# Depthwise convolution of two channel blocks on TensorE, one more C product on VectorE and a single buffer for step size times x, in the state-space layer of a decoder kernel

## What is computed

```
h = _rms(x, norm_w[i])
xz = jnp.einsum('bld,ed->ble', h, W_in[i])
xi, z = jnp.split(xz, 2, axis=-1)
xp = jnp.pad(xi, ((0, 0), (dc - 1, 0), (0, 0)))
xc = conv_b[i] + sum((xp[:, k:k + L, :] * conv_w[i][:, k] for k in range(dc)))
xc = _silu(xc)
dbc = jnp.einsum('bld,ed->ble', xc, W_x[i])
delta, Bm, Cm = jnp.split(dbc, [rk, rk + n], axis=-1)
delta = jax.nn.softplus(jnp.einsum('blr,dr->bld', delta, W_dt[i]) + b_dt[i])
deltaA = jnp.exp(delta[..., None] * A)
BX = (delta * xc)[..., None] * Bm[:, :, None, :]
_, hs = jax.lax.associative_scan(combine, (deltaA, BX), axis=1)
y = jnp.einsum('bldn,bln->bld', hs, Cm) + D[i] * xc
out = jnp.einsum('bld,ed->ble', y * _silu(z), W_out[i])
x = x + out
```

## Time and profile before

| | us |
|---|---|
| median of three runs | 1399.4 |
| profiled execution | 1391.54 |
| span of the profiled execution | 1389.8 |
| state-space stage in it | 380 to 1077 |

### The profile page before, as it was taken

One profiled execution on the slowest core, in us unless ns is written; L12 is line 12 of the kernel. 1 busy time (PEld: TensorE's weight loads), 2 busy tenths in 40 slices (PEclk: granted clock), 3 DMA queues, 4 the chain that ended last, 5 costly groups with the idle time before them and its releaser, 6 DMA issues.

```text
span 1389.8 us, 17376 instructions
## 1 busy us (share of the span) xinstructions
PE 1138.0 (82%) x5946; PEld 665.0 (48%) x5946; DVE 1119.4 (81%) x1662; ACT 791.7 (57%) x1749; POOL 862.7 (62%) x745
## 2 busy tenths in 40 slices
PE   6688888878579898987988889888787788888774
PEld 2455555544234454544545445454443455556544
DVE  3677777575699999999999999999999167876558
ACT  1355555564367567666676666766653056566653
POOL 4700000100499898998989989999898245445404
PEclk9799999988779899999999999999999889999975
DMA  6000002000510504106041060320500300010000
GB/s 210 11 12 12 12 12 68 1 1 3 196 37 22 210 0 167 40 1 232 0 146 61 1 231 1 116 90 0 191 1 0 107 16 16 17 31 2 1 0 24
DMA packets 21028, 79.88 MB, mean 57 GB/s; under 512 B 4273, under 2 KB 7417, under 8 KB 19961
## 3 DMA queue, kind: packets, MB, share of 16 engines
q1 hardware_dynamic: 20942, 78.79, 16.4%
HBM read 77.55 MB, written 1.23 MB: 57 GB/s over the span
## 4 chain that ended last, share of the span: by engine, by line
PE 29%; POOL 29%; DVE 26%; ACT 9%; issue 5%; DMA 1%; SPq 0%; DVEq 0%; POOLq 0%; ACTq 0%
PE ps L522 27%; POOL arena L1586 17%; POOL arena L1598 9%; DVE ps L1668 5%; DVE hstat L952 4%; ACT arena L739 3%; DVE arena L1673 3%; DVE arena L1671 2%; PE ps L586 2%; DVE arena L1633 2%; DVE arena L940 1%; ACT L517 1%; ACT ps L1486 1%; ACT arena L749 1%; POOL arena L1575 1%
## 5 line engine op out<-in xcount | busy, mean ns | idle before, releaser
L522 PE MATMUL ps<-arena 128*32 128x100 f32 (+11 forms) x3188 | 476.6, 378 | 73.9 <-ACT arena L739 29.3
L522 PE MATMUL ps<-arena,ident 128*128 128x400 f32 x1024 | 395.4, 538 | 99.8 <-POOL arena L1598 65.0
L1586 POOL TENSOR_TENSOR arena<-arena 128x1600 f32<-128x1600 f32 x128 | 456.6, 3580 | 9.1 <-DVE ps L1668 7.8
L1486 ACT ACTIVATE ps<-arena 128x400 f32<-128x400 f32 x512 | 282.9, 589 | 174.2 <-DVE arena L1671 121.0
L522 PEld LDWEIGHTS ps<-arena 128*32 128x32 f32 (+10 forms) x3188 | 243.3, 145 | 257.3 <-issue 106.7
L522 PEld LDWEIGHTS ps<-arena,ident 128*128 128x128 f32 x1024 | 201.5, 203 | 282.2 <-issue 67.7
L1668 DVE TENSOR_TENSOR_SCAN ps<-ps,arena 128x800 f32<-128x800 f32 x160 | 291.2, 1820 | 12.0 <-ACT ps L1486 9.6
L497 POOL TENSOR_SCALAR stat<-stat 100x1 f32<-100x1 f32 (+1 forms) x44 | 8.9, 201 | 317.0 <-DVE stat L478 315.9
L739 ACT ACTIVATE arena<-ps,hstat 100x361 f32<-100x361 f32 x256 | 143.5, 563 | 106.7 <-DVE hstat L952 106.5
L1598 POOL TENSOR_TENSOR arena<-arena 128x1600 f32<-128x1600 f32 x48 | 171.5, 3573 | 15.4 <-DVE arena L1673 15.4
L1673 DVE TENSOR_TENSOR_SCAN arena<-ps,arena 128x800 f32<-128x800 f32 x96 | 168.5, 1805 | 5.6 <-POOL arena L1586 4.8
(11 more groups left out here) (182 smaller groups left out, 1048.9 us busy)
## 6 DMA issues: line engine op xcount, KB each, us to landing
arena<-bc_scratch SPq DMA_DIRECT2D x64, 800.0 KB, 6.8
arena<-in_ctxT SPq DMA_DIRECT2D x16, 361.0 KB, 4.2
arena<-in_w_in SPq DMA_DIRECT2D x4, 1024.0 KB, 6.4
arena<-in_expT SPq DMA_DIRECT2D x1, 2048.0 KB
arena<-in_w_out SPq DMA_DIRECT2D x4, 512.0 KB, 3.3
arena<-in_mask SPq DMA_DIRECT2D x8, 141.0 KB
wo<-in_L_Wo SPq DMA_DIRECT2D x2, 512.0 KB
arena<-in_xT SPq DMA_DIRECT2D x1, 800.0 KB
```

The source lines that it names most:

```text
L522: return nc.tensor.matmul(outp, lhsT, rhs, start=first, stop=last)
L1486: last = nc.scalar.activation(psf[:, half_at(k) + j * GT:half_at(k) + (j + 1) * GT], delta[g][:, c], ACT.Exp, scale=aneg[:, l % 2, n:n + 1])
L1586: nc.gpsimd.tensor_tensor(bx[:, unit % BX].rearrange("p (j t) -> p j t", j=SEGMENT), bbc[:, nq].rearrange("p (j t) -> p j t", j=SEGMENT), ...
```

## The change

Three edits. (1) For rounds 1 to 7, the convolution of blocks 0 and 1 is done by TensorE: ScalarE builds, once per inner layer, eight diagonal matrices (`am_taps`: identity scaled by a tap, four behind unit 6 and four behind unit 7), copies raw X0 and X1 into `xc` (`am_raw_x`), TensorE multiplies by the four tap matrices of each block into two new products Y0 and Y1 (`pm_conv`, behind unit 9's work, ahead of reduce(8)), and ScalarE writes them with the bias back to `xc` (`am_conv_out`, u = 10). VectorE convolves only blocks 2 and 3 (u = 10). (2) Unit 9's product with C moves from GpSimd to VectorE: eleven of 16 units instead of ten. (3) `dx` has one buffer; `gm_delta` waits until the round before has read its block.

```
-DVE_C = (0, 3, 4, 5, 7, 10, 11, 13, 14, 15)
+DVE_C = (0, 3, 4, 5, 7, 9, 10, 11, 13, 14, 15)
...
-    "vC": (9, 10),
+    "aG": (6, 7),
+    "pY": 10,
+    "aY": 10,
+    "vC": 10,
...
-        PREP = ["T0", "T1"] + [f"X{e}" for e in IN_ORDER] + ["DB"] + [f"D{c}" for c in range(CD)]
+        PREP = (["T0", "T1"] + [f"X{e}" for e in IN_ORDER[:CD + 2]] + ["Y0", "Y1"] + [f"X{e}" for e in IN_ORDER[CD + 2:]]
+                + ["DB"] + [f"D{c}" for c in range(CD)])
...
+        def pm_conv(pe, m, c):
+
+            pe.wait_ge(m_taps, m // G + 1)
+            n = f"Y{c}"
+            p_read(pe, m, f"X{c}")
+            p_free(pe, m, n)
+            y3 = ps[:, p_bank(m, n), 0:GT].rearrange("p (b t) -> p b t", b=GB)
+            x3 = xc[m % G][:, c].rearrange("p (b t) -> p b t", b=GB)
+            for s in range(DC):
+                last = mm(y3[:, :, s:S], taps[:, c, DC - 1 - s], x3[:, :, 0:S - s], s == 0, s == DC - 1)
+            last.then_inc(m_full, 1)
...
                                 pm_in(pe, m + 1, e)
+                            if e == 1 and u == AT["pY"]:
+                                pm_conv(pe, m + 1, 0)
+                                pm_conv(pe, m + 1, 1)
...
+        def am_raw_x(act, m, g, c):
+
+            n = f"X{c}"
+            p_full(act, m, n)
+            nc.scalar.activation(xc[g][:, c], ps[:, p_bank(m, n), 0:GT], ACT.Copy).then_inc(p_done(m, n), 1)
+
+        def am_conv_out(act, m, g, c):
+
+            n = f"Y{c}"
+            p_full(act, m, n)
+            nc.scalar.activation(xc[g][:, c], ps[:, p_bank(m, n), 0:GT], ACT.Identity, bias=cvb[:, c:c + 1],
+                                 scale=1.0).then_inc(p_done(m, n), 1)
+
+        def am_taps(act, m, l, c):
+
+            act.wait_ge(ld_w, 80 * (l + 1))
+            if m and c == 0:
+                p_full(act, m, "Y1")
+            for k in range(DC):
+                last = nc.scalar.activation(taps[:, c, k], ident[:, :], ACT.Identity,
+                                            scale=cvw[:, DC * c + k:DC * c + k + 1])
+            if c == 1:
+                last.then_inc(m_taps, 1)
...
-                for c in range(CD):
-                    p_read(act, m, f"X{c}")
+                for n in ("Y0", "Y1", "X2", "X3"):
+                    p_read(act, m, n)
...
-            nc.gpsimd.tensor_tensor(dx[g][:, c], delta[g][:, c], xc[g][:, c], ALU.mult).then_inc(m_dx, 1)
+                pool.wait_ge(m_bx, UNITS * (m - 1) + NQ * (c + 1))
+            nc.gpsimd.tensor_tensor(dx[:, c], delta[g][:, c], xc[g][:, c], ALU.mult).then_inc(m_dx, 1)
...
-                        for k in range(2):
-                            if u == AT["vC"][k]:
-                                vm_conv(dve, m + 1, ng, 2 * k)
+                        if u == AT["vC"]:
+                            vm_conv(dve, m + 1, ng, 2)
```

More of the change, by code:

```diff
@@ L251, in decoder @@
         bbc, cbc = mam.take(NQ, SEGMENT * GT), mam.take(NQ, SEGMENT * GT)
-        delta, dx, xc, sz = [None, None], [None, None], [None, None], [None, None]
-        delta[1], dx[1], dx[0] = (mam.take(CD, GT) for _ in range(3))
+        delta, xc, sz = [None, None], [None, None], [None, None]
+        delta[1] = mam.take(CD, GT)
+        taps = mam.take(2, DC, P)
+        mam.at += CD * GT - 2 * DC * P
+        dx = mam.take(CD, GT)
         bx = mam.take(BX, SEGMENT * GT)
@@ L1105, in decoder @@
         m_root, m_conv, m_soft = sem("m_root"), sem("m_conv"), sem("m_soft")
+        m_taps = sem("m_taps")
         ROUNDS = G * NL
         IN_ORDER = [*range(CD, 2 * CD), *range(CD)]
-        PREP = ["T0", "T1"] + [f"X{e}" for e in IN_ORDER] + ["DB"] + [f"D{c}" for c in range(CD)]
+        PREP = (["T0", "T1"] + [f"X{e}" for e in IN_ORDER[:CD + 2]] + ["Y0", "Y1"] + [f"X{e}" for e in IN_ORDER[CD + 2:]]
+                + ["DB"] + [f"D{c}" for c in range(CD)])
         ORDER = []
@@ L1356, in am_raw @@
             p_full(act, 0, n)
-            nc.scalar.activation(dx[0][:, c], ps[:, p_bank(0, n), 0:GT], ACT.Copy).then_inc(p_done(0, n), 1)
+            nc.scalar.activation(dx[:, c], ps[:, p_bank(0, n), 0:GT], ACT.Copy).then_inc(p_done(0, n), 1)
         def am_tap(act, c):
             p_read(act, 0, f"X{c}")
-            nc.scalar.activation(xc[0][:, c], dx[0][:, c], ACT.Identity, bias=cvb[:, c:c + 1],
+            nc.scalar.activation(xc[0][:, c], dx[:, c], ACT.Identity, bias=cvb[:, c:c + 1],
                                  scale=cvw[:, DC * c + DC - 1:DC * c + DC]).then_inc(m_acc, 1)
@@ L1511, in mam_act @@
                             am_z(act, m + 1, ng, c)
-                    for c in range(CD):
+                    for c in range(2):
+                        if u == AT["aC"][c]:
+                            am_raw_x(act, m + 1, ng, c)
+                        if u == AT["aG"][c] and (m == 0 or g == 1):
+                            am_taps(act, m, l + g, c)
+                    for c in range(2):
+                        if u == AT["aY"]:
+                            am_conv_out(act, m + 1, ng, c)
+                    for c in range(2, CD):
                         if u == AT["aC"][c]:
@@ L1588, in gm_bx @@
                 bbc[:, nq].rearrange("p (j t) -> p j t", j=SEGMENT),
-                dx[m % G][:, c].rearrange("p (o t) -> p o t", o=1).to_broadcast([P, SEGMENT, GT]),
+                dx[:, c].rearrange("p (o t) -> p o t", o=1).to_broadcast([P, SEGMENT, GT]),
                 ALU.mult).then_inc(m_bx, 1)
@@ L1624, in vm_conv @@
         def vm_conv(dve, m, g, c0):
-            dve.wait_ge(m_acc, CD * m + c0 + 2)
+            dve.wait_ge(m_acc, 2 * m + CD)
             for s in range(1, DC):
@@ L1646, in vm_conv_first @@
                     a3 = xc[0][:, c].rearrange("p (b t) -> p b t", b=GB)[:, :, s:S]
-                    x3 = dx[0][:, c].rearrange("p (b t) -> p b t", b=GB)[:, :, 0:S - s]
+                    x3 = dx[:, c].rearrange("p (b t) -> p b t", b=GB)[:, :, 0:S - s]
                     k = DC * c + DC - 1 - s
```

## The result

The changed kernel takes 1419.8 us in the median of five runs (1416.9 to 1428.8); the kernel before, run beside it, 1399.4 (1395.3 to 1405.1). The ratio is 1.018 [1.0139, 1.0221]: slower by 1.8%, or 25 us [19, 31]. The two medians alone lie 20.4 us (1.5%) apart, inside that interval. The forecast was 1424.5 (1410 to 1440), that is +25.1 us. The profiled execution of after took 1428.75 us (span 1427.0), the longest of its five; that of before 1391.54.

A forecast was written before the change was run, and what follows sets the result against it. VectorE was taken as the stage's bound, with TensorE's chain to X2 ending last; 4.4 + 6 x 3.38 + 0.4 = 25.1 us on the 1399.4 us median gives 1424.5 us, range 1410 to 1440.

The forecast's parts named there:

- Taps 5.30 us: On TensorE behind the D term: eight tap matmuls, sixteen rows at 0.336 us scaled to 394 columns, take 5.30 us.
- VectorE's wait 5.3: Round 3, ahead of the remaining convolution: VectorE is ready at 700.1 and waits until 705.39, 5.3 us instead of 0.5.
- Round 0: TensorE had almost no idle time there, so the convolution starts at 440.57 instead of 436.14: +4.4 us.
- Rounds 1 to 6: Round 3 stands for these six: less VectorE work, longer wait for the convolution, +3.38 us each.
- Round 7: Prepares nothing; VectorE gains 2.07 us of work, its 1.42 us wait for a B product goes: +0.4 us.
- GpSimd's idle time: State-space stage: a sign in the profile after, GpSimd's idle time grows by some 7 us a round.
- ScalarE's Y passes and the taps' building: On ScalarE: Y passes lie in its 6.60 us wait for X2; building taken as zero, at most 10 us.
- `gm_delta` at no cost: On GpSimd: the new wait on its own earlier B products taken as zero, at most 2.8 us for 28.
- Slow taps: Rival, TensorE: broken PSUM runs or a clock drop make taps dearer; 1461 at twice the price, 1446 milder; chance 0.10.
- second rival: VectorE's work decides, 1392 us, as TensorE takes the taps in idle time; break-even at taps of 3.29 us; chance 0.08.
- Waits given back: Rival: VectorE's other stage waits, 9.6 us for decays and 4.8 for B products, could go: 1410 us; chance 0.12.
- The range's upper end: Whole kernel: 1440 us, given as the upper bound and half of the milder slow case.

The follow-up runs named there:

- single-`dx` run: The kernel before with only the single buffer for step size times x and its wait on GpSimd; ratio 1.0022 [0.9999, 1.0044] to the kernel before.
- one-block kernel: Changed kernel with TensorE convolving only block 0, X2 and X3 ahead of reduce(8), ten C products on VectorE; ratio 0.9896 [0.987, 0.9923] to the kernel before.

## Why the prediction was right, point by point

The steps, with the forecast first and the trace of after second:

- Taps 5.30 us; 5.29. Distance from the D term to X2 8.66; 8.65. From X2 to the convolution 3.61; 3.61. VectorE's wait 5.3; 5.23.
- Round 0 +4.4 us; +4.5. Rounds 1 to 6 +3.38 each; +3.63 in the mean (+3.38 over rounds 1 to 3 alone). Round 7 +0.4; +0.1. Sum 25.1; 26.4. The chain gives 3.35 of the 3.63; that the other waits of the stage changed by only +1.0 us in all is in part luck, since in other kernels here they moved by several us.
- GpSimd's idle time was to grow by some 7 us a round. It must wait for the scans behind the long wait: its wait for VectorE's scans is 57.3 us in 12, before 7.8 in 12, so 7.1 in each of seven rounds. The groups of the page (busy us, mean ns, idle before):

```profile
L1642 POOL TENSOR_TENSOR arena<-arena 128x1600 f32<-128x1600 f32 x128 | 456.2, 3580 | 58.5 <-DVE ps L1724 57.3
...
L1689 DVE SCALAR_TENSOR_TENSOR arena<-ps,arena 128x396 f32<-128x396 f32 (+2 forms) x42 | 24.4, 622 | 36.4 <-ACT arena L1445 35.9
```

- ScalarE's Y passes and the taps' building at no cost: right in rounds 1 to 7, where the building's waits are ahead of the long one. In round 0 there was something: a wait of 2.38 us at unit 7 where 1.19 stood. The four scalings stand ahead of the decays that it needs; these and GpSimd's B product, to which the view puts the wait, end at the same time. It lies ahead of the long wait too and doesn't come out.
- `gm_delta` at no cost: right, by the single-`dx` run.
- Slow taps (0.10) did not come. The forms of TensorE's instructions in the stage (busy us, mean ns):

```profile
L528 PE MATMUL ps<-arena 128*128 128x400 f32 x316 | 117.2, 502 | 0.0
...
L528 PE MATMUL ps<-arena 128*128 128x396 f32 x28 | 11.6, 496 | 0.0
...
L528 PE MATMUL ps<-arena 128*128 128x388 f32 x28 | 11.4, 488 | 0.0
```

A tap of 4 x 97 columns, written in four broken runs, has a mean of 488 ns, one of 4 x 99 columns 496, and the unbroken 400 columns 502. Start to start, the sixteen rows of the taps took 5.29 us. The row was the right guide. The Trainium skill's note on cachelines (SBUF — State Buffer, section on Door 1), that a non-contiguous PSUM pattern slows matmuls, does not show here, for four long runs.

Where it was wrong, though the total didn't show it:

- **The second rival's point of balance.** It said that the kernel breaks even with X2 at 698.40 + 1.37 = 699.77, so at taps of 3.29 us, as if VectorE's saved 1.37 us could pay for a later X2. They can't: that work lies ahead of the wait. With X2 at 699.77 the convolution starts 3.61 us behind, at 703.38, which is 1.37 later than before. Break-even is X2 at 698.40, so taps of 1.85 us. Nor could X2 start by 696.5, as the gain of this rival needs: the prediction itself has reduce(8) waiting for GpSimd until about 695.5, and its 2.69 us come ahead of X2. With taps of 1.35 us the kernel was no faster than before. So this edit, at this place, had no way to gain by shorter taps.
- **The shares of the cause.** The sum put the whole loss to the taps. Moving reduce(8) from ahead of X2 to behind it, with all taps left in, took three quarters of it away. The taps are as much to blame as what they push.
- **Waits given back** (0.12), taken as 14.4 us or nothing. In after they were not given back (11.2 us for decays, 9.6 before). In the run with the eleventh product alone 7.4 us of them were, in the one-block kernel 3.7. The rival was real in size up to a half (7.4 and 0.4 of 14.4 us) and bound to the wrong condition: in these traces it goes with TensorE's full rate at reduce(12), not with relief for GpSimd, which after had as well. The kernel with X2 and X3 ahead of reduce(8) stands between: reduce(12) at its full rate in three of seven rounds, 6.8 us of waits for decays.
- **The range's upper end.** The terms that it names don't give 1440: 1424.5 + 10 + 2.8 is 1437.3, and with half of 21 us it is 1447.8. The bound is a choice between the two.

Open: why reduce(12) is slow in most rounds of one kernel and not in another's. The load of the DMA engines doesn't tell them apart (their share was 0.95 in the slow stretch of round 3 and 0.85 in the same place of round 5). No run here sets it apart.

## What to carry to other kernels

Price work that is moved to an engine with slack by its place in that engine's list: what stands between its inputs and the product that the bound engine waits for next. Here 1.85 us of slack stood before the place and 5.3 us went in. Then move what is waited for ahead of other work, and hand over only as much as lets both engines arrive together; with unit 9's C product back on GpSimd, that turned +1.8% into -1.0%. Before moving an operand of VectorE from PSUM to SBUF to free a bank, look whether GpSimd is busy beside it.

## What the hardware showed unexpected

- An instruction of VectorE on 396 columns takes 0.62 us with one operand in PSUM and 6.5, 7.5 or 11.8 us (14.69 less 2.92) with both in SBUF, when GpSimd has a run of instructions without pause: it ended 0.4 us behind the end of the whole run, not of the instruction that was under way. Its time shows as busy, not as a wait.
- TensorE's granted clock isn't told by the idle time ahead of a row. In the kernel before, the same eight rows at the same place behind 2.2 us without work took 4.62 us in round 3 and 2.93 us in round 5; at the earlier trace rows the granted clock was 0.64, so part of the row ran at 1.2 GHz, and in round 5 it was 1.00 from 894.80 to 897.70. Each slow one stood 9 us ahead of 1.4 us that VectorE waited.
